# Second phase of a three-phase decoder layer: logits computed three query tiles ahead, the masked minimum placed ahead of the low part

## The chip, the cores and the metric

The kernel runs on one core of a Trainium2 chip. The metric is device time in microseconds (us) from one launch, median of repeated runs. The engines are named as the profile names them: PE is TensorE (PEld its weight loads), DVE is VectorE, ACT is ScalarE, POOL is GpSimd, and SP issues most of the transfers. Each engine runs its own list of instructions in the order in which the code issues them; semaphores tie the lists together.

## The reference, cut to what matters

The layer has three parts over 16 batches of 512 tokens with 512 features: a linear attention with a short convolution, a cross attention against a memory sequence, and a gated recurrence over the batch axis. The change is in the second part alone. With `xn` and `mn` the normalised tokens and memory, 4 query heads and one key/value head of 128 features:

```python
q = jnp.einsum('BTD,NDH->BTNH', xn, q_w)
kv = jnp.einsum('BSD,cKDH->cBSKH', mn, kv_w)
k, v = (kv[0], kv[1])
q = _apply_rope(q, q_pos) * HEAD_DIM ** (-0.5)
k = _apply_rope(k, k_pos)
logits = jnp.einsum('BTKGH,BSKH->BKGTS', q, k, preferred_element_type=jnp.float32)
masked = jnp.where(mem_mask[:, None, None, None, :], logits, MASK_FILL)
probs = jax.nn.softmax(masked, axis=-1).astype(x.dtype)
enc = jnp.einsum('BKGTS,BSKH->BTKGH', probs, v).reshape(B, T, NUM_HEADS, HEAD_DIM)
return jnp.einsum('BTNH,NHD->BTD', enc, out_w)
```

Before it, the memory's rows are scaled by the inverse root of their mean square; the sums of squares for that are the "memory's squares" of the change.

## The kernel before, in words

Every matrix operand is kept as two fp32r tensors, a high part (rounded on ACT) and a low part (the rest, subtracted on DVE), and `product` (lines 126 to 130, its three matmuls at L130, L131 and L132) multiplies high by high, high by low and low by high. The three phases follow each other; `phase_b` is the second.

**The pipeline.** `pipeline3` runs `step(s, new, old, fin)` for s = 0 to 17. In step s, batch s (`new`) has its keys, values and queries made, batch s-1 (`old`) goes through the softmax, and batch s-2 (`fin`) is finished and projected out. The memory of batch s+1 (`after`) is prepared at the end of step s. Steps 2 to 15 have all three batches; step 1 has no `fin`, step 16 no `new`.

**The slots.** A step has J = 16 slots, j = 0 to 15, one for each tile of 128 queries by 512 keys of `old` (4 heads by 4 tiles). Each engine has its own loop over j, and the order in these loops is written out by hand. What a tile goes through:
- PE `logits(b, j)`: one product into one of two PSUM banks, `logit_banks[j % 2]`. It waits until the tile that stood there two before has been read: `earlier(top_sb, b, j, 2)`.
- DVE `masked(b, j)` (L1393, L1394): adds the mask, takes the negated minimum, and writes the tile to one of four places in SBUF (`soft`, `SLOTS = 4`). Its second instruction, the read of the accumulator, posts `top_sb`.
- ACT `exp` (L1248), DVE `one_over` (L1383, a reciprocal), POOL `normalise` (L1200).
- PE `turn_p(j)` (L1580): four transposes into the single PSUM bank `pT_bank`. It waits for `normalise` and until the low part of the tile before has been read out of that bank.
- ACT `p_high` (L1257) and DVE `p_low` (L1402) split that bank, and PE `encode` (tile b_e) multiplies four such tiles by the values.

In a slot of PE `logits` comes first, then the work of that slot (keys and values at slots 0 and 2, the output at 3 to 6, `encode`, the queries at 8, 9, 11 and 12, the turning of the memory at 13 and 14), and `turn_p(j)` last. On DVE a slot is `one_over(j+1)`, `p_low(j-1)`, `masked(j+2)`, then the rest. The memory of `after` is turned on PE in slots 13 and 14, rounded on ACT in slots 14 and 15 (`memory_high`, L1128), and its low parts are made on DVE in slots 14 and 15 (`memory_low`, L1132), each waiting for its high part.

Two of the lines that matter below, in PE's `logits` and in DVE's `masked`:

```python
if free := earlier(top_sb, b, j, 2):
    pe.wait_ge(*free)
```

Of the kernel before, what the change touches and what calls it, by code (L numbers as in the profile page):

```python
# [189 lines left out]
class Kernel:  # L190
# [728 lines left out]
    def phase_b(self, ctx):  # L919
# [2 lines left out]
        BIG = 2.0 ** 100  # L922
        HALF = HD // 2
        J = H * T
        SLOTS = 4
        with ExitStack() as held:
            sb = lambda n, s, d=F32: self.sb(ctx, f"b_{n}", s, d)
            ev = lambda n, per=1, unit=1: Event(ctx, nc, f"b_{n}", per, unit)
# [226 lines left out]
            def tile(b, j):  # L1155
                return (b * J + j) % SLOTS

# [85 lines left out]
            def scalar(act):  # L1243
                def step(s, new, old, fin):
# [56 lines left out]
                    after = new.b + 1 if following(new, B) else None  # L1301
                    for j in range(J):
# [46 lines left out]
                        if s == 0 and 2 <= j <= 5:  # L1349
                            output_weight_high(act, j - 2)  # L1350
                        if after:
                            if 3 <= j <= 6:
                                square(act, after, j - 3)
                            if j == 8:
                                mem_apply(act, after, 0)
                                mem_apply(act, after, 1)
                            if j == 10 or j == 11:
                                mem_apply(act, after, j - 8)
# [17 lines left out]
            def vector(dve):  # L1376
                dve.wait_ge(params.sem, params.upto(0))

                def step(s, new, old, fin):
                    def one_over(b, j):  # L1380
                        at = tile(b, j)
                        dve.wait_ge(p_exp.sem, p_exp.upto(b, j))
                        dve.reciprocal(one_in_sum[:, at:at + 1], row_sum[:, at:at + 1]).then_inc(sum_one.sem, sum_one.unit)  # L1383

                    def masked(b, j):

                        at = tile(b, j)
                        dve.wait_ge(logit_ps.sem, logit_ps.upto(b, j))
                        if free := earlier(pT_ps, b, j, SLOTS):
                            dve.wait_ge(*free)  # L1390
                        if j == 0:
                            dve.wait_ge(mask_f.sem, mask_f.upto(b))
                        dve.memset(carrier[:, at:at + 1], 0.0)  # L1393
                        dve.tensor_tensor_reduce(out=soft[:, at, :], in0=logit_banks[j % 2][:, :], in1=mask_row[b % 2][:, :],  # L1394
                                                 scale=-1.0, scalar=3e38, op0=ALU.add, op1=ALU.min,
                                                 accum_out=minus_top[:, at:at + 1]).then_inc(top_sb.sem, top_sb.unit)
# [58 lines left out]
                    after = new.b + 1 if following(new, B) else None  # L1455
                    for j in range(J):
                        if old and j < J - 1:
                            one_over(old.b, j + 1)
                        if new and j == J - 1:
                            one_over(new.b, 0)  # L1460
                        if old and j >= 1:
                            p_low(old.b, j - 1)
                        if fin and j == 0:
                            p_low(fin.b, J - 1)
                        if after and j == 15:
                            memory_low(dve, s, after, 2)
                            memory_low(dve, s, after, 3)
                        if old and j < J - 2:
                            masked(old.b, j + 2)
                        if new and j >= J - 2:  # L1470
                            masked(new.b, j - J + 2)
                        if fin:
                            if j == 0:
                                enc_low(fin.b, 2)
# [83 lines left out]
            def tensor(pe):  # L1558
                def step(s, new, old, fin):
# [75 lines left out]
                        mm.then_inc(q_ps.sem, q_ps.unit)  # L1635

                    for j in range(J):
                        if old and j < J - 2:
                            logits(old.b, j + 2)
                        if s == 0 and j == J - 2:  # L1640
                            pe.wait_ge(self.a_x1.sem, self.a_x1.upto(B - 1))
                        if new and j >= J - 2:
                            logits(new.b, j - J + 2)
                        if new and j == 0:
                            keys_values(0)
                        if fin and j == 1:
# [654 lines left out]
```

## Time and profile before

| what | us |
|---|---|
| median of 3 runs (3152.20 to 3154.09) | 3153.61 |
| the profiled execution | 3155.96 |
| its span, first to last instruction | 3154.2 |
| PE busy | 3115.6 (99%) |
| DVE busy | 1778.2 (56%) |
| ACT busy | 1297.7 (41%) |
| POOL busy | 836.5 (27%) |
| TensorE clock granted, mean | 0.997 |

The profiled execution has 1.8 us outside its span and is 2.35 us above the median of the runs. The chain that ended last is PE for 96% of the span. The second phase runs from about 924 us to about 1895 us of the span. A full step of it takes 60.69 us. In timelines a row's first number is the start in us from the span's start, the second its length; "x4" merges four instructions in a row; square brackets at the end give the engine's idle time before the row and what ended it. "PEclk" is the granted clock, 1.00 for 2.4 GHz and 0.50 for 1.2 GHz.

### The profile page before, as it was taken

The page shows a single profiled execution, that of the slowest core. Times are in us where ns is not written, and L with a number is a line of the kernel's source. Part 1 is how long each engine was busy: PE and PEld are TensorE (multiplying, and loading weights), DVE is VectorE, ACT ScalarE, POOL GpSimd, SP SyncE. Part 2 cuts the span into 40 slices and gives each one's busy share as a digit, 9 for nine tenths or more (in the row PEclk, how much of TensorE's full clock was granted, in tenths as well). Part 3 has the DMA queues.
Part 4 walks back from the last instruction along what each step waited for, and adds up shares of the span by engine and source line. Part 5 has one row for each costly group of instructions (what it writes and reads, how often), then busy time and mean ns, then how long its engine had stood idle before and what let it go on. Part 6 is the DMA issues. An engine that isn't in the chain of part 4 may idle for free.

```text
span 3154.2 us, 41122 instructions
## 1 busy us (share of the span) xinstructions
PE 3115.6 (99%) x15828; PEld 2630.9 (83%) x15828; DVE 1778.2 (56%) x3901; ACT 1297.7 (41%) x2475; POOL 836.5 (27%) x699
## 2 busy tenths in 40 slices
PE   8999999999989999999999989999999999999999
PEld 7888888888878888888888878888888888888887
DVE  6666665757577877777787766232232232221355
ACT  4333333333446766766666653222222212221243
POOL 0101010100146666666666650000000000000144
PEclk9999999999999999999999999999999999999999
DMA  3121121212222112211211232000001000010386
GB/s 111 41 72 50 48 73 41 81 41 94 72 99 81 57 68 78 72 69 55 95 69 55 80 103 86 27 27 27 27 31 50 27 27 27 27 54 17 122 292 227
DMA packets 118802, 220.76 MB, mean 70 GB/s; under 512 B 7504, under 2 KB 13648, under 8 KB 118608
## 3 DMA queue, kind: packets, MB, share of 16 engines
q1 hardware_dynamic: 118608, 218.14, 20.2%
q8 instruction: 126, 2.06, 0.3%
q14 instruction: 68, 0.56, 0.1%
HBM read 152.06 MB, written 66.06 MB: 69 GB/s over the span
## 4 chain that ended last, share of the span: by engine, by line
PE 96%; DVE 1%; ACT 1%; issue 1%; DMA 0%; POOL 0%; SPq 0%; DVEq 0%; ACTq 0%
PE c_p L132 11%; PE c_p L131 11%; PE c_p L130 11%; PE a_p L130 6%; PE a_p L132 5%; PE a_p L131 5%; PE b_n L132 5%; PE b_n L130 5%; PE b_n L131 5%; PE b_t L1580 3%; PE d_p L130 2%; PE d_p L132 2%; PE d_p L131 2%; PE a_r L130 2%; PE a_r L132 2%; PE a_r L131 2%
## 5 line engine op out<-in xcount | busy, mean ns | idle before, releaser
L1200 POOL TENSOR_SCALAR b_soft<-b_soft,b_one_in_sum 128x512 f32<-128x512 f32 x256 | 401.2, 1568 | 299.8 <-DVE b_one_in_sum L1383 299.8
L1800 ACT ACTIVATE c_gate<-c_p,c_bias 128x512 f32<-128x512 f32 x180 | 124.2, 690 | 718.3 <-PE c_p L132 718.3
L1834 DVE TENSOR_TENSOR c_gate<-c_gate,c_gate 128x512 f32<-128x512 f32 x64 | 44.3, 692 | 524.0 <-ACT c_gate L1800 524.0
L1402 DVE TENSOR_TENSOR b_p_lo<-b_t,b_p_hi 128x512 fp32r<-128x512 f32 x256 | 175.1, 684 | 159.8 <-ACT b_p_hi L1257 157.2
L1248 ACT ACTIVATE b_soft<-b_soft,b_minus_top 128x512 f32<-128x512 f32 x256 | 185.2, 723 | 180.7 <-DVE b_minus_top L1394 176.1
L344 POOL TENSOR_TENSOR kept_scale<-c_ln_ve,minus_half 128x4 f32<-128x4 f32 x16 | 16.1, 1009 | 898.5 <-DVE c_ln_ve L336 898.5
L551 ACT ACTIVATE a_elu<-a_p 128x512 f32<-128x512 f32 x128 | 76.5, 598 | 353.0 <-PE a_p L132 353.0
L344 POOL TENSOR_TENSOR a_ln_sc<-a_ln_ve,minus_half 128x4 f32<-128x4 f32 x16 | 16.3, 1017 | 695.6 <-DVE a_ln_ve L336 695.6
L1257 ACT ACTIVATE b_p_hi<-b_t 128x512 fp32r<-128x512 f32 x256 | 151.7, 592 | 108.6 <-PE b_t L1580 108.6
L1394 DVE CUSTOM_DVE_ANT_0 b_soft<-b_l,b_mask_row 128x512 f32<-128x512 f32 x256 | 175.2, 684 | 0.0
L1580 PE MATMUL b_t<-ident,b_soft 128*128 128x128 f32 x1024 | 155.7, 275 | 10.7 <-DVE b_p_lo L1402 9.6
L2024 POOL TENSOR_TENSOR d_x<-d_x,d_y 128x512 f32<-128x512 f32 x60 | 79.8, 1332 | 260.5 <-ACT d_y L2041 260.4
L1580 PEld LDWEIGHTS b_t<-ident,b_soft 128*128 128x128 f32 x1024 | 123.0, 142 | 29.7 <-DVE b_p_lo L1402 14.6
L130 PE MATMUL b_l<-b_k_hi,b_q_hi 128*128 128x512 f32 x256 | 122.7, 479 | 0.0
L667 DVE SCALAR_TENSOR_TENSOR a_q<-a_p,a_elu 128x512 f32<-128x512 f32 x64 | 44.2, 691 | 134.3 <-ACT a_elu L553 134.3
L1836 DVE TENSOR_TENSOR c_gate<-c_gate,c_c_f 128x512 f32<-128x512 f32 x64 | 44.2, 691 | 122.8 <-ACT c_gate L1800 122.8
L130 PE MATMUL a_p<-a_Wk_hi,a_xT_hi 128*128 128x512 f32 x256 | 105.3, 411 | 0.1
L130 PE MATMUL a_p<-a_Wv_hi,a_xT_hi 128*128 128x512 f32 x256 | 104.1, 407 | 0.0
L130 PE MATMUL a_r<-a_Wp_hi,a_z_hi 128*128 128x512 f32 x256 | 102.9, 402 | 0.0
L130 PE MATMUL b_e<-b_p_hi,b_v_hi 128*128 128x512 f32 x256 | 101.0, 395 | 0.8 <-DVE b_enc_lo L1407 0.8
L132 PE MATMUL b_l<-b_k_hi,b_q_lo 128*128 128x512 f32 x256 | 101.6, 397 | 0.0
L130 PE MATMUL c_p<-c_nT_hi,c_wf_hi 128*128 128x512 f32 x256 | 101.0, 395 | 0.0
(286 smaller groups left out, 9614.8 us busy)
## 6 DMA issues: line engine op xcount, KB each, us to landing
a_res<-in_x SPq DMA_DIRECT2D x16, 1024.0 KB, 5.9
x<-a_res SPq DMA_DIRECT2D x16, 1024.0 KB, 5.2
b_mem<-in_ctx SPq DMA_DIRECT2D x16, 1024.0 KB, 5.3
b_x<-x SPq DMA_DIRECT2D x16, 1024.0 KB, 5.6
b_res<-x SPq DMA_DIRECT2D x16, 1024.0 KB, 5.6
x<-b_res SPq DMA_DIRECT2D x16, 1024.0 KB, 4.5
c_x<-x SPq DMA_DIRECT2D x16, 1024.0 KB, 5.8
d_x<-x SPq DMA_DIRECT2D x16, 1024.0 KB, 6.6
```

The source lines that it names most:

```text
L130: pe.matmul(out, stationary.high, moving.high, start=first, stop=False)
L131: pe.matmul(out, stationary.high, moving.low, start=False, stop=False)
L132: return pe.matmul(out, stationary.low, moving.high, start=False, stop=last)
L551: act.activation(elu[:, u % 2, :], bank[:, :], ACT.Relu, scale=-1.0).then_inc(elu_exp.sem, elu_exp.unit)
L1200: pool.tensor_scalar(soft[:, at, :], soft[:, at, :], one_in_sum[:, at:at + 1], None, ALU.mult).then_inc(p_norm.sem, p_norm.unit)
L1248: act.activation(soft[:, at, :], soft[:, at, :], ACT.Exp, bias=minus_top[:, at:at + 1], scale=-1.0, accum_out=row_sum[:, at:at + 1]).then_ ...
L1257: act.activation(p[h % 2].high[:, :, t * P:(t + 1) * P], pT_bank[:, :].rearrange("p (i s) -> p i s", i=T), ACT.Copy).then_inc(p_hi.sem, p_ ...
L1394: dve.tensor_tensor_reduce(out=soft[:, at, :], in0=logit_banks[j % 2][:, :], in1=mask_row[b % 2][:, :], scale=-1.0, scalar=3e38, op0=ALU.a ...
L1402: dve.tensor_tensor(part.low, pT_bank[:, :].rearrange("p (i s) -> p i s", i=T), part.high_f32(), ALU.subtract).then_inc(p_lo.sem, p_lo.unit)
L1580: mm = pe.transpose(pT_bank[:, i * P:(i + 1) * P], soft[:, tile(old.b, j), i * P:(i + 1) * P], self.ident[:, :])
L1800: act.activation(gate[j % 2][i][:, :], gating.banks[(3 * j + i) % 6][:, :], ACT.Tanh if g == "c" else ACT.Sigmoid, bias=added[:, i, j:j + ...
L2024: pool.tensor_tensor(x[old.par][:, t, :], x[old.par][:, t, :], y[:, t % 2, :], ALU.add).then_inc(out_sb.sem, out_sb.unit)
```

## The change

Four edits, all in `phase_b`:
- PE computes `logits` three tiles ahead instead of two (`AHEAD = 3`). The first tiles of the new batch thus stand in slots 13, 14 and 15 of its step. There are still two PSUM banks for the logits and four places in `soft`.
- DVE's `masked(j+2)` stands ahead of `p_low(j-1)` in slots 0 to 14. In slot 15 `masked(new, 1)` stays behind `memory_low`.
- In step 1 alone, ACT's squares of the memory stand in slot 2 (three) and slot 3 (one) instead of one in each of slots 3 to 6.
- `memory_low` in slot 15 is written at another place of the loop, with the same neighbours as before.

```diff
--- before.py
+++ after.py
@@ -922,7 +922,7 @@
         BIG = 2.0 ** 100
         HALF = HD // 2
         J = H * T
-        SLOTS = 4
+        SLOTS, AHEAD = 4, 3
         with ExitStack() as held:
             sb = lambda n, s, d=F32: self.sb(ctx, f"b_{n}", s, d)
             ev = lambda n, per=1, unit=1: Event(ctx, nc, f"b_{n}", per, unit)
@@ -1349,7 +1349,13 @@
                         if s == 0 and 2 <= j <= 5:
                             output_weight_high(act, j - 2)
                         if after:
-                            if 3 <= j <= 6:
+                            if s == 1 and j == 2:
+                                square(act, after, 0)
+                                square(act, after, 1)
+                                square(act, after, 2)
+                            if s == 1 and j == 3:
+                                square(act, after, 3)
+                            if s != 1 and 3 <= j <= 6:
                                 square(act, after, j - 3)
                             if j == 8:
                                 mem_apply(act, after, 0)
@@ -1458,17 +1464,19 @@
                             one_over(old.b, j + 1)
                         if new and j == J - 1:
                             one_over(new.b, 0)
+                        if old and j < J - 2:
+                            masked(old.b, j + 2)
+                        if new and j == J - 2:
+                            masked(new.b, 0)
                         if old and j >= 1:
                             p_low(old.b, j - 1)
                         if fin and j == 0:
                             p_low(fin.b, J - 1)
-                        if after and j == 15:
+                        if after and j == J - 1:
                             memory_low(dve, s, after, 2)
                             memory_low(dve, s, after, 3)
-                        if old and j < J - 2:
-                            masked(old.b, j + 2)
-                        if new and j >= J - 2:
-                            masked(new.b, j - J + 2)
+                        if new and j == J - 1:
+                            masked(new.b, 1)
                         if fin:
                             if j == 0:
                                 enc_low(fin.b, 2)
@@ -1635,12 +1643,12 @@
                         mm.then_inc(q_ps.sem, q_ps.unit)
 
                     for j in range(J):
-                        if old and j < J - 2:
-                            logits(old.b, j + 2)
-                        if s == 0 and j == J - 2:
+                        if old and j < J - AHEAD:
+                            logits(old.b, j + AHEAD)
+                        if s == 0 and j == J - AHEAD:
                             pe.wait_ge(self.a_x1.sem, self.a_x1.upto(B - 1))
-                        if new and j >= J - 2:
-                            logits(new.b, j - J + 2)
+                        if new and j >= J - AHEAD:
+                            logits(new.b, j - J + AHEAD)
                         if new and j == 0:
                             keys_values(0)
                         if fin and j == 1:
```

PE at the seam of two steps, before. The first two rows are the last `turn_p` of step 1; the names b_l0 and b_l1 are the two logit banks, and b_n is the bank that takes keys and values:

```order
L1580 MATMUL b_t0<-ident_49,b_soft_183 128x128 [waits b_p_norm,b_p_lo]
L1580 MATMUL b_t0<-ident_49,b_soft_183 128x128 x3
L130 MATMUL b_l0<-b_k1_hi_188,b_q_hi_175 128x512 [waits b_top_sb]
L131 MATMUL b_l0<-b_k1_lo_189,b_q_hi_175 128x512
L132 MATMUL b_l0<-b_k1_hi_188,b_q_lo_176 128x512
L130 MATMUL b_n2<-b_kvw_hi_170,b_nT_hi_172 128x256 [waits b_memT_lo]
L131 MATMUL b_n2<-b_kvw_lo_171,b_nT_hi_172 128x256
```

and after, at the same seam:

```order
L1588 MATMUL b_t0<-ident_49,b_soft_183 128x128 [waits b_p_norm,b_p_lo]
L1588 MATMUL b_t0<-ident_49,b_soft_183 128x128 x3
L130 MATMUL b_l1<-b_k1_hi_188,b_q_hi_175 128x512 [waits b_top_sb]
L131 MATMUL b_l1<-b_k1_lo_189,b_q_hi_175 128x512
L132 MATMUL b_l1<-b_k1_hi_188,b_q_lo_176 128x512
L130 MATMUL b_n2<-b_kvw_hi_170,b_nT_hi_172 128x256 [waits b_memT_lo]
L131 MATMUL b_n2<-b_kvw_lo_171,b_nT_hi_172 128x256
```

The product behind the last `turn_p` is tile 2 in bank b_l0 before, and tile 3 in bank b_l1 after. The wait on b_top_sb is for tile 0 before and for tile 1 after; keys and values are behind it in both.

DVE in slot 14 of step 1 (`one_over`, `p_low`, then `masked` of the new batch's tile 0), before:

```order
L1383 RECIPROCAL b_one_in_sum_212<-b_row_sum_211 128x1 [waits b_p_exp]
L1402 TENSOR_TENSOR b_p1_lo_180<-b_t0,b_p1_hi_179 128x4x128 [waits b_p_hi]
L1393 MEMSET b_carrier_209 128x1 [waits b_mask_f,b_pT_ps,b_logit_ps]
L1394 ISA b_soft_183,b_minus_top_210<-b_l0,b_mask_row1_206 128x512
L1394 ISA b_minus_top_210 128x1
```

and after:

```order
L1389 RECIPROCAL b_one_in_sum_212<-b_row_sum_211 128x1 [waits b_p_exp]
L1399 MEMSET b_carrier_209 128x1 [waits b_mask_f,b_pT_ps,b_logit_ps]
L1400 ISA b_soft_183,b_minus_top_210<-b_l0,b_mask_row1_206 128x512
L1400 ISA b_minus_top_210 128x1
L1408 TENSOR_TENSOR b_p1_lo_180<-b_t0,b_p1_hi_179 128x4x128 [waits b_p_hi]
```

`masked` (the rows with b_carrier, b_soft and b_minus_top) has moved ahead of `p_low` (b_p1_lo), and both are behind `one_over` (b_one_in_sum). The next slot of DVE, slot 15 of step 1, after:

```order
L1389 RECIPROCAL b_one_in_sum_212<-b_row_sum_211 128x1 [waits b_p_exp]
L1408 TENSOR_TENSOR b_p1_lo_180<-b_t0,b_p1_hi_179 128x4x128 [waits b_p_hi]
L1132 TENSOR_TENSOR b_nT_lo_173<-b_n0,b_nT_hi_172 128x512 [waits b_memT_hi]
L1132 TENSOR_TENSOR b_nT_lo_173<-b_n1,b_nT_hi_172 128x512 [waits b_memT_hi]
L1399 MEMSET b_carrier_209 128x1 [waits b_pT_ps,b_logit_ps]
L1400 ISA b_soft_183,b_minus_top_210<-b_l1,b_mask_row1_206 128x512
L1400 ISA b_minus_top_210 128x1
```

These rows stand in the same order before: `masked` of tile 1, the one that PE's first product of the next step waits for after the change, is behind `p_low` and the two `memory_low` (b_nT_lo).

ACT in step 1, from `p_high` of slot 2 on, before:

```order
L1257 ACTIVATE b_p0_hi_177<-b_t0 128x4x128 [waits b_pT_ps]
L1248 ACTIVATE b_soft_183,b_row_sum_211<-b_soft_183,b_minus_top_210 128x512 [waits b_top_sb]
L1257 ACTIVATE b_p0_hi_177<-b_t0 128x4x128 [waits b_pT_ps]
L1270 ACTIVATE b_v1_hi_192<-b_n0 128x256 [waits b_kv_ps]
L1248 ACTIVATE b_soft_183,b_row_sum_211<-b_soft_183,b_minus_top_210 128x512 [waits b_top_sb]
L1031 ACTIVATE b_unused_sq0_207,b_sumsq_213<-b_mem_181 128x512 [waits b_sq,b_ms,b_mem_in]
L1257 ACTIVATE b_p0_hi_177<-b_t0 128x4x128 [waits b_pT_ps]
L1278 ACTIVATE b_nT_hi_172<-b_n1 128x512 [waits b_kv_ps,b_xT_ps]
```

and after:

```order
L1257 ACTIVATE b_p0_hi_177<-b_t0 128x4x128 [waits b_pT_ps]
L1248 ACTIVATE b_soft_183,b_row_sum_211<-b_soft_183,b_minus_top_210 128x512 [waits b_top_sb]
L1031 ACTIVATE b_unused_sq0_207,b_sumsq_213<-b_mem_181 128x512 [waits b_sq,b_ms,b_mem_in]
L1031 ACTIVATE b_unused_sq1_208,b_sumsq_213<-b_mem_181 128x512 [waits b_sq]
L1031 ACTIVATE b_unused_sq0_207,b_sumsq_213<-b_mem_181 128x512 [waits b_sq]
L1257 ACTIVATE b_p0_hi_177<-b_t0 128x4x128 [waits b_pT_ps]
L1270 ACTIVATE b_v1_hi_192<-b_n0 128x256 [waits b_kv_ps]
L1248 ACTIVATE b_soft_183,b_row_sum_211<-b_soft_183,b_minus_top_210 128x512 [waits b_top_sb]
```

The first three squares (b_unused_sq) now stand in a row between an `exp` and the next `p_high`.

## Rows read from the trace of the kernel before

**Rows 1.** Busy time by stage. Columns are named in the first line; (x) counts instructions.
```profile
core 0: us, PE busy (x) PEld busy (x) DVE busy (x) ACT busy (x) POOL busy (x), PEclk, DMA share, GB/s
924.00:955.00 31.00, 24.83 (x146) 20.05 (x145) 26.17 (x77) 20.58 (x48) 24.00 (x22) 0.94 0.20 67
955.00:1825.00 870.00, 870.00 (x4865) 746.16 (x4864) 683.72 (x1858) 580.32 (x1238) 563.41 (x470) 1.00 0.20 70
1825.00:1895.00 70.00, 61.55 (x321) 48.66 (x320) 47.14 (x126) 38.64 (x82) 33.44 (x23) 0.95 0.35 121
1895.00:3150.00 1255.00, 1253.24 (x5695) 1040.91 (x5693) 418.46 (x716) 314.06 (x524) 95.97 (x76) 1.00 0.20 68
```

**Rows 2.** Waits of PE in 924 to 955: total, times, longest.
```profile
PE b_t L1580 <- DVE b_p_lo L1402: 3.2, 4, 1.5
```

**Rows 3.** Waits of PE in 1825 to 1895.
```profile
PE b_t L1580 <- DVE b_p_lo L1402: 6.3, 6, 1.6
```

**Rows 4.** Timeline of PE at the seam of steps 1 and 2.
```profile
980.50 0.60 PE L1580 MATMUL b_t<-ident,b_soft 128*128 128x128 f32 x4
...
983.02 0.60 PE L1580 MATMUL b_t<-ident,b_soft 128*128 128x128 f32 x4
983.38 0.48 PE L130 MATMUL b_l<-b_k_hi,b_q_hi 128*128 128x512 f32 x1
```

**Rows 5.** Timeline of ACT at the same seam.
```profile
981.14 0.60 ACT L1257 ACTIVATE b_p_hi<-b_t 128x512 fp32r<-128x512 f32 x1
981.63 1.08 ACT L1128 ACTIVATE b_nT_hi<-b_n 128x512 fp32r<-128x512 f32 x2
```

**Rows 6.** Timeline of DVE at the same seam.
```profile
981.77 0.69 DVE L1402 TENSOR_TENSOR b_p_lo<-b_t,b_p_hi 128x512 fp32r<-128x512 f32 x1
982.38 1.28 DVE L1132 TENSOR_TENSOR b_nT_lo<-b_n,b_nT_hi 128x512 fp32r<-128x512 f32 x2
...
984.19 0.08 DVE L1394 DVE_READ_ACCUMULATOR2_ANT b_minus_top<- 128x1 f32 x1
```

**Rows 7.** Timeline of PE and DVE at the seam of steps 14 and 15.
```profile
1772.30 0.48 PE L130 MATMUL b_l<-b_k_hi,b_q_hi 128*128 128x512 f32 x1
...
1773.12 0.09 DVE L1394 DVE_READ_ACCUMULATOR2_ANT b_minus_top<- 128x1 f32 x1
```

**Rows 8.** Timeline at the seam of steps 0 and 1.
```profile
928.62 0.28 PE L130 MATMUL b_n<-b_kvw_hi,b_nT_hi 128*128 128x256 f32 x1
...
930.50 0.08 DVE L1394 DVE_READ_ACCUMULATOR2_ANT b_minus_top<- 128x1 f32 x1
...
933.16 0.55 PE L1580 MATMUL b_t<-ident,b_soft 128*128 128x128 f32 x3 [1.09 <-POOL b_soft L1200]
```

**Rows 9.** Timeline in step 1, from one turn_p to the next.
```profile
944.07 0.69 DVE L1402 TENSOR_TENSOR b_p_lo<-b_t,b_p_hi 128x512 fp32r<-128x512 f32 x1 [0.38 <-ACT b_p_hi L1257]
...
944.81 0.66 PE L1580 MATMUL b_t<-ident,b_soft 128*128 128x128 f32 x4 [1.50 <-DVE b_p_lo L1402]
...
945.41 0.72 ACT L1248 ACTIVATE b_soft<-b_soft,b_minus_top 128x512 f32<-128x512 f32 x1 [0.89 <-DVE b_minus_top L1394]
...
946.13 0.61 ACT L1031 ACTIVATE b_unused_sq<-b_mem 128x512 bf16<-128x512 f32 x1
...
946.75 0.58 ACT L1257 ACTIVATE b_p_hi<-b_t 128x512 fp32r<-128x512 f32 x1
...
948.10 0.69 PE L1580 MATMUL b_t<-ident,b_soft 128*128 128x128 f32 x2 [0.38 <-DVE b_p_lo L1402]
```

**Rows 10.** Timeline of PE in step 16, turn_p of slots 11 to 15.
```profile
1876.59 0.66 PE L1580 MATMUL b_t<-ident,b_soft 128*128 128x128 f32 x4 [1.32 <-DVE b_p_lo L1402]
...
1879.27 1.12 PE L1580 MATMUL b_t<-ident,b_soft 128*128 128x128 f32 x4 [1.32 <-DVE b_p_lo L1402]
...
1882.74 1.05 PE L1580 MATMUL b_t<-ident,b_soft 128*128 128x128 f32 x4
...
1889.84 0.66 PE L1580 MATMUL b_t<-ident,b_soft 128*128 128x128 f32 x4 [0.98 <-DVE b_p_lo L1402]
```

## The prediction

> **What bounds the kernel now.** The page first: PE is busy for 99% of the span and the chain that ended last is PE for 96% of it. So a change pays only if it takes idle time from PE, and costs whatever idle time it gives to PE. Next, the second phase by stage [rows 1]. Between 955 and 1825 us PE is busy for 870.00 of 870.00 us at a granted clock of 1.00. The two ends are different: 6.17 us idle in 924 to 955 (step 0's end and step 1), 8.45 us idle in 1825 to 1895 (step 15's end and step 16), and the mean clock is 0.94 and 0.95 there. The third view is the waits of PE in those two stretches: 3.2 and 6.3 us of them end with p_low [rows 2, 3], that is, turn_p waits for its single PSUM bank. The last view is the timeline at the places that the order of instructions points at, below.
>
> The reader is to see two things: all that the change can win lies in two stretches that together hold 14.6 us of idle time, and in the 870 us between them it can only lose.
>
> **Part 1: the seam of two steps.** PE's first instruction of a step is, after the change, the product of tile 3. It waits for the read of tile 1, since both use the second logit bank. DVE reads tile 1 in slot 15, and that order is untouched: p_low, two memory_low, then masked. Before, PE's first product is tile 2 and waits for tile 0, read a slot earlier.
>
> When is PE there, and when is tile 1 read? At the seam of steps 1 and 2, PE is done with turn_p(15) and starts its product at 983.38 [rows 4]. DVE's read of the accumulator, which posts tile 1, ends at 984.19 + 0.08 = 984.27 [rows 6]. A matmul that waits for DVE starts 0.05 us after DVE's instruction ends (944.07 + 0.69 = 944.76, then 944.81) [rows 9]. So PE starts at 984.32 instead of 983.38: 0.94 us idle.
>
> Can tile 1 be read earlier once the products are earlier? Its product is, by a whole slot, but that is not what holds it. What does is turn_p(14) at 980.50 [rows 4]: p_high follows at 981.14, memory_high at 981.63 [rows 5], p_low at 981.77, memory_low twice from 982.38 (0.60 apart), and masked behind them [rows 6]. The chain starts on PE in slot 15 itself, and PE's work from turn_p(14) to the step's end is as long as before (one product, two parts of encode, turn_p: 2.88 us from 980.50 to 983.38), against 3.77 us for the chain. A stall does not cure the next one: all engines shift together, as the period of 60.69 us a step (983.38 to 1772.30 over 13 steps [rows 4, 7]) is the same for all now. And nothing on PE that could run stands ahead of the waiting product: keys and values, behind it, are held up too.
>
> How often? The last seam with memory work, steps 14 and 15, has the same distance: 1773.12 + 0.09 against 1772.30 [rows 7], 0.91 + 0.05 = 0.96. There are 14 such seams, after steps 1 to 14; step 15 prepares no memory, and the seam after step 0 is counted in part 2. Price 14 x 0.94 = 13.2 us. PE has no idle time there in which it could vanish, so all of it is on the path. Bounds: 14 x 0.94 from below as long as the chain stands; above, 14 x 1.1 = 15.4 if the restart costs another 0.1 to 0.2 on a few. If the wait weren't there: 0.
>
> Other waits on the logit banks in a step are hidden: the read of a tile stands one slot of DVE before the product that needs it, with nothing as long as the memory's work ahead of it, and the shortest slot of PE in a full step is 2.5 us long (980.50 to 983.02 [rows 4]). I take 0.
>
> **Part 2: step 0's end and step 1.** The seam of steps 0 and 1 has the same wait, larger. Keys and values started at 928.62, and turn_p(0) waited 1.09 us for POOL until 933.16 [rows 8]; that makes 933.16 - 1.09 - 928.62 = 3.45 us of work with some waiting of its own in it. After the change PE has the product of tile 3 ahead of them, which waits for tile 1 until 930.50 + 0.08 + 0.05 = 930.63 [rows 8]; with 0.7 us for the product and 2.9 to 3.4 for the rest turn_p(0) is at 934.3 to 934.8, where 1.1 us of waiting was before. That is a loss of 1.1 to 1.6 us. I take 1.1.
>
> Then the gain. In slots 4 to 6 of step 1 one turn_p follows the other after 948.10 - 944.81 = 3.29 us, and the loop between them is p_low, masked, exp (945.41), square (946.13), p_high (946.75), p_low, turn_p [rows 9]. Masked ahead of p_low, and the squares out of these slots, cut it to turn_p to p_high 0.64, p_high to p_low 0.63 [rows 4 to 6], p_low to turn_p 0.74 [rows 9]: 2.01 us. But DVE has four instructions of some 0.61 each in such a slot (masked, p_low, the tokens' low part, a query's sum or the like), so I take 2.5. Three intervals give 3 x 0.79 = 2.4 us. Against it stand 0.5 us because the three squares in a row (each holds ACT for 0.62, 946.13 to 946.75) put 1.9 us ahead of p_high in slot 2, where turn_p(3) also waits for DVE's normalising of the tokens. Sum: 1.1 + 0.5 - 2.4 = -0.8 us. Bounds: the idle time of 6.17 and 0.06 x 31 x 1 = 1.9 us of clock are all that can be won; lost can be 1.6 + 1.9 + a second spell of the low clock, 1.7. From -8 to +5; the value lies near zero because DVE, not PE, is what these slots then wait for.
>
> **Part 3: step 16.** Here masked ahead of p_low does what it did in step 1. From slot 11 to slot 13 turn_p follows at 2.68 and 3.47 us [rows 10], with waits of 1.32 each for p_low. The floor is again 2.01. Slot 11 has the same wait as slot 12, so the three intervals are 2.68 + 2.68 + 3.47 = 8.8 us and become 6.0: 2.8 us. Of the 8.45 - 2 x 1.32 = 5.8 us of idle time that is left, and of slots 14 and 15 (7.10 us from 1882.74 to 1889.84), I take about four tenths, 2.4 us: part of it waits for the gate weights' low parts, for which the change does nothing, and where DVE is late masked now delays p_low by 0.61. Sum -5.2 us. Bounds: 0, and 8.45 + 0.05 x 70 = 11.9.
>
> **Part 4: edits at no cost.** The squares of the other steps, the normalising, all transfers and POOL's list are where they were. Masked ahead of p_low in the full steps delays p_low by at most 0.61 where DVE is late, and turn_p behind it has 0.56 us to spare even in the shortest slot (p_low ends at 982.46, turn_p starts at 983.02 [rows 4, 6]), where masked moves nothing: 0. Without that cover it would be rival D.
>
> **The sum** for the profiled execution: 3155.96 + 13.2 - 0.8 - 5.2 = 3163.2. The median of the runs is 2.35 us lower: 3160.8.
>
> **A rule to weigh.** In 1895 to 3150 the clock stays at 1.00 with 1.8 us of idle time in all; in 924 to 955, with 6.17 us idle in 31, it is 0.94 [rows 1]. The Trainium skill, page "TensorE: Matmul & The Clock Gate", section "A second HAM failure mode: psum-queue depth-cycling", says that short, frequent idles of PE between groups of matmuls over PSUM banks can make the clock swing between its two levels. By that rule the seams, a bank's wait once a step, would pay twice; rival C prices it. The trace speaks against it here: one idle of 0.94 in 61.6 us is far rarer than what stands in 924 to 955.
>
> **The rivals.**
> A. The seam's wait isn't there, or is small: masked of tile 1 ends before PE arrives, because what feeds DVE comes forward more than I see. For it: the product of tile 1 and exp of tile 0 both come earlier. Against: the chain runs through turn_p(14) [rows 4 to 6]. Time 3153.6 - 6.0 = 3147.6, faster than before. It decides if slot 15's chain shrinks by 0.9 of its 3.77 us.
> B. The stalls are there, but the ends give more: all loops reach 2.01, the low clock of both stretches (1.9 and 3.5 us) goes. Start -3, end -9: 3153.6 + 13.2 - 12 = 3154.8, within 0.2%.
> C. Every seam costs a spell of the lower clock. In 924 to 955 the 0.06 of 31 us are 1.9 us lost; 14 x 1.9 = 26 more: about 3187.
> D. DVE is the next bound in the full steps, since p_low is late: turn_p waits in a slot or two of each step, 14 x 0.3 = 4 more: 3165.
>
> **How the numbers follow.** The forecast (seams plus small gains at the ends) 0.68, with a range of its own from 3157.5 to 3164.5; A 0.11, B 0.12, C 0.03, D 0.06. 0.2% is 6.3 us, about what a measurement of this kernel can tell from no change: slower begins at 3159.9. Of the forecast 0.11 lies below that, so slower is 0.57 + 0.03 + 0.06 = 0.66; A is half beyond the bound, faster 0.06; the rest, 0.28, is the same. The range 3155 to 3166 takes in the forecast's own, part of B and D, and leaves out A and C.
>
> **What the profile after would show.** Waits of PE b_l for DVE b_minus_top, 14 of about 0.9 us and one of 2 to 3 us at some 928, where before there is none; PE busy 870 of some 883 us in the middle stretch; steps of 61.6 us instead of 60.7; turn_p in slots 11 to 13 of step 16 some 2.0 us apart; step 1 about as long as before. Wrong I am if PE shows no wait for b_minus_top at the seams, or if the middle keeps its 60.69 us a step.

## The result: 3163.4 us, slower by 0.3%, and the profile after

| | before | after |
|---|---|---|
| median of 8 runs, us | 3153.61 (3151.58 to 3154.09) | 3163.44 (3162.83 to 3165.43) |
| ratio, 95% interval | | 1.0032 [1.0023, 1.0041] |
| profiled execution, us | 3155.96 | 3163.65 |
| its span, us | 3154.2 | 3161.9 |

The changed kernel is slower by 9.8 us where the forecast said 7.2; by the interval of the ratio the difference lies between 7.3 and 12.9 us. The page of the profile after, its first lines:

```profile
span 3161.9 us, 41122 instructions
...
PE 3114.1 (98%) x15828; PEld 2628.3 (83%) x15828; DVE 1785.1 (56%) x3901; ACT 1291.4 (41%) x2475; POOL 836.6 (26%) x699
```

PE does the same 15828 instructions and is busy for 3114.1 us, 1.5 less than before, so the time went into idle time of PE. Where it stands, by the stages of [rows 1] (the columns are those), with the bounds moved to where the stages now lie:

```profile
924.00:955.00 31.00, 25.45 (x162) 20.89 (x161) 27.34 (x83) 21.22 (x51) 25.72 (x24) 1.00 0.23 81
955.00:1838.00 883.00, 873.07 (x4858) 746.23 (x4858) 688.54 (x1855) 573.58 (x1238) 562.77 (x469) 1.00 0.20 68
1838.00:1906.00 68.00, 60.11 (x332) 48.10 (x331) 50.13 (x133) 39.63 (x84) 33.49 (x23) 1.00 0.35 124
1906.00:3160.00 1254.00, 1249.90 (x5676) 1038.39 (x5674) 415.61 (x706) 312.47 (x521) 94.91 (x76) 1.00 0.20 69
```

The middle, where PE had no idle time at all, now has 9.93 us of it. The waits of PE between 955 and 1840 (total, times, longest) name it:

```profile
PE b_l L130 <- DVE b_minus_top L1400: 9.9, 14, 0.7
```

and between 924 and 955, beside the waits for p_low [rows 2], one for the read:

```profile
PE b_t L1588 <- DVE b_p_lo L1408: 3.2, 5, 1.0
PE b_l L130 <- DVE b_minus_top L1400: 2.3, 1, 2.3
```

The seam of steps 1 and 2 again, first PE, then ACT and DVE, the places of [rows 4 to 6]:

```profile
978.90 0.60 PE L1588 MATMUL b_t<-ident,b_soft 128*128 128x128 f32 x4
...
981.42 0.60 PE L1588 MATMUL b_t<-ident,b_soft 128*128 128x128 f32 x4
982.73 0.50 PE L130 MATMUL b_l<-b_k_hi,b_q_hi 128*128 128x512 f32 x1 [0.71 <-DVE b_minus_top L1400]
```

```profile
979.54 0.60 ACT L1257 ACTIVATE b_p_hi<-b_t 128x512 fp32r<-128x512 f32 x1 [0.43 <-PE b_t L1588]
980.03 1.08 ACT L1128 ACTIVATE b_nT_hi<-b_n 128x512 fp32r<-128x512 f32 x2
```

```profile
980.17 0.69 DVE L1408 TENSOR_TENSOR b_p_lo<-b_t,b_p_hi 128x512 fp32r<-128x512 f32 x1 [0.58 <-ACT b_p_hi L1257]
980.78 1.28 DVE L1132 TENSOR_TENSOR b_nT_lo<-b_n,b_nT_hi 128x512 fp32r<-128x512 f32 x2
981.98 0.69 DVE L1400 CUSTOM_DVE_ANT_0 b_soft<-b_l,b_mask_row 128x512 f32<-128x512 f32 x1
...
982.59 0.08 DVE L1400 DVE_READ_ACCUMULATOR2_ANT b_minus_top<- 128x1 f32 x1
```

From turn_p(14) to the posted read is 978.90 to 982.67, 3.77 us, the same as before. PE's product would follow turn_p(15) after 0.36 us [rows 4], at 981.78, and starts at 982.73, 0.95 later. The row shows only 0.71 of it as idle, since the end of the transposes ahead of it is modelled. A reader who adds up the idle time (9.9 us in 14 waits) is some 3.8 us short of what the waits cost (13.7 us, below).

To see the cost whole, I measure from one turn_p to the next, all from the starts of turn_p in the traces. The mark for the first seam is an instruction of step 0 on DVE, first before, then after. On DVE nothing ahead of it was changed. On PE the product of tile 0 now stands ahead of it in time, but that doesn't move the mark: it comes 6.61 us after the first BATCH_NORM_STATS2 of its group before (917.91) and 6.62 after (917.53).

```profile
924.52 0.68 DVE L326 BATCH_NORM_STATS2 b_ln_st<-b_x 128x6 f32<-128x512 f32 x1
```

```profile
924.15 0.68 DVE L326 BATCH_NORM_STATS2 b_ln_st<-b_x 128x6 f32<-128x512 f32 x1
```

A star says that PE's clock fell in that part of that profile; "again" is a second profile of the kernel before, and e1 to e8 are the experiments below. A step goes from turn_p(15) to turn_p(15).

| us | before | again | after | e7 | e3 | e2 | e1 | e8 |
|---|---|---|---|---|---|---|---|---|
| mark to turn_p(0) of step 1 | 8.64 | 8.65 | 9.79 | 9.79 | 8.64 | 9.20 | 8.66 | 8.63 |
| step 1, turn_p(0) to (15) | 49.87* | 51.26* | 47.48 | 50.05 | 52.30* | 47.46 | 48.03 | 48.01 |
| one of steps 2 to 14 | 60.69 | 60.69 | 61.66 | 61.65 | 60.80 | 61.06 | 60.77 | 60.76 |
| step 15 | 60.14 | 60.15 | 61.20 | 61.23 | 60.81 | 60.60 | 60.71 | 60.28 |
| step 16 | 57.75* | 55.80 | 53.32 | 55.65 | 56.70* | 53.34 | 52.71 | 53.31 |
| turn_p(15) of step 16 to the end | 1264.34 | 1264.35 | 1264.35 | 1264.38 | 1264.36 | 1264.35 | 1264.38 | 1264.35 |

After against before, in the order of the rows: +1.15 at the first seam, -2.4 in step 1, 13 x 0.97 = +12.6, +1.1 in step 15, -4.4 in step 16, 0 behind it. With the mark itself 0.4 earlier this is +7.7, the difference of the spans (3161.9 - 3154.2).

### The profile page after: what moved, and what is told of

Its sections match the earlier page's. It is cut to its first block, busy times and chain, and to the rows that moved or that the text cites. A ratio compares the mean times of both kernels' runs of the same rounds, so it can differ in the third digit from the quotient of the medians.

```text
span 3161.9 us, 41122 instructions
## 1 busy us (share of the span) xinstructions
PE 3114.1 (98%) x15828; PEld 2628.3 (83%) x15828; DVE 1785.1 (56%) x3901; ACT 1291.4 (41%) x2475; POOL 836.6 (26%) x699
## 4 chain that ended last, share of the span: by engine, by line
PE 96%; DVE 2%; ACT 1%; issue 1%; DMA 0%; SPq 0%; DVEq 0%; ACTq 0%
PE c_p L132 11%; PE c_p L130 11%; PE c_p L131 11%; PE a_p L130 5%; PE a_p L132 5%; PE a_p L131 5%; PE b_n L132 5%; PE b_n L130 5%; PE b_n L131 5%; PE b_t L1588 3%; PE d_p L130 2%; PE d_p L132 2%; PE d_p L131 2%; PE a_r L130 2%; PE a_r L132 2%; PE a_r L131 2%
## 5 line engine op out<-in xcount | busy, mean ns | idle before, releaser
L130 PE MATMUL b_l<-b_k_hi,b_q_hi 128*128 128x512 f32 x256 | 122.7, 479 | 12.5 <-DVE b_minus_top L1400 12.2
L130 PE MATMUL c_p<-c_nT_hi,c_wc_hi 128*128 128x512 f32 x256 | 101.1, 395 | 0.0
```

The lines of the kernel that those rows point to most:

```text
L130: pe.matmul(out, stationary.high, moving.high, start=first, stop=False)
```

## The experiments

The kernels are named e1 to e8. "ratio" is to the kernel before, from runs on the same chip, with its 95% interval.

### e1: tile 1 read ahead of the low parts in slot 15

```diff
-                        if new and j == J - 2:
-                            masked(new.b, 0)
+                        if new and j >= J - 2:
+                            masked(new.b, j - J + 2)
                         if old and j >= 1:
                             p_low(old.b, j - 1)
 ...
-                        if new and j == J - 1:
-                            masked(new.b, 1)
```

> The changed kernel, but in slot 15 DVE reads tile 1 of the new batch ahead of p_low and of the two memory_low. Theory (the 9.8 us are 14 seams of 0.97 us in which PE waits for that read, 13.6 us, less what the ends give): the waits of PE b_l for b_minus_top go from 14 to 0 in the middle, a step is 60.7 us again, the seam of steps 0 and 1 waits about 0.9 instead of 2.3 us, and the time is 3163.4 - 13.6 - 1.4 = 3148.4, faster than before by 5. Rival 1 (the products three ahead cost by themselves, through the two banks or the order on PE): 3163 stays. Rival 2 (the wait only moves: memory's low parts come 0.6 to 1.2 us later and keys and values wait for them at the seam): a wait of PE b_n for b_nT_lo of 0.3 or more per seam, 3153 or above.

Measured: 3149.21 us (11 runs), ratio 0.9988 [0.9979, 0.9996], 14.2 less than after. The waits of PE for b_minus_top are gone between 955 and 1825, and the first one fell from 2.3 to 0.9 us, which costs nothing (8.66 us from the mark to turn_p(0)). Of the 1.13 us that are won there step 1 gives back 0.55 (48.03 instead of 47.48), since turn_p(1) now comes 2.75 us after turn_p(0) instead of 2.01; together with steps that are 0.08 longer than 60.69 this makes up the 0.8 us by which 3148.4 was missed. All waits of PE from 924 to 955:

```profile
PE b_t L1586 <- DVE b_p_lo L1408: 3.8, 5, 1.4
PE b_l L130 <- DVE b_minus_top L1400: 0.9, 1, 0.9
```

DVE at the seam, where the read now stands ahead of p_low and memory_low:

```profile
977.04 0.69 DVE L1400 CUSTOM_DVE_ANT_0 b_soft<-b_l,b_mask_row 128x512 f32<-128x512 f32 x1
977.66 0.09 DVE L1400 DVE_READ_ACCUMULATOR2_ANT b_minus_top<- 128x1 f32 x1
977.66 0.69 DVE L1408 TENSOR_TENSOR b_p_lo<-b_t,b_p_hi 128x512 fp32r<-128x512 f32 x1
978.26 1.28 DVE L1132 TENSOR_TENSOR b_nT_lo<-b_n,b_nT_hi 128x512 fp32r<-128x512 f32 x2
```

So the place of that one read is the cause of the loss, and with it moved the kernel beats both others, the one before by 0.12% (0.04 to 0.21).

### e2: one memory_low ahead of the read instead of two

```diff
                         if after and j == J - 1:
                             memory_low(dve, s, after, 2)
-                            memory_low(dve, s, after, 3)
                         if new and j == J - 1:
                             masked(new.b, 1)
+                        if after and j == J - 1:
+                            memory_low(dve, s, after, 3)
```

> The changed kernel, but only one of the two memory_low of slot 15 stays ahead of the read of tile 1. Theory: the chain to the read is one DVE instruction shorter (0.60 us), so the seam's cost falls from 0.97 to 0.37 us: 14 x 0.60 = 8.4 us less, and 0.6 less at the first seam, 3163.4 - 9.0 = 3154.4; a step is 61.1 us. Rival 1: no change, 3163. If the wait were set by something other than this chain (ACT, the product of tile 1), it would stay near 0.97 or vanish altogether.

Measured: 3155.07 us (11 runs), ratio 1.0003 [0.9994, 1.0012]. A step takes 61.06 us, 0.37 over 60.69; taking 0.60 us out of the chain took 0.60 out of the stall. PE and then DVE at the seam of steps 1 and 2:

```profile
981.59 0.60 PE L1589 MATMUL b_t<-ident,b_soft 128*128 128x128 f32 x4
982.30 0.50 PE L130 MATMUL b_l<-b_k_hi,b_q_hi 128*128 128x512 f32 x1
```

```profile
982.16 0.08 DVE L1400 DVE_READ_ACCUMULATOR2_ANT b_minus_top<- 128x1 f32 x1
```

The product starts 0.71 after turn_p(15) instead of 0.36, 0.06 after the read ends, yet the row has no bracket: the stall of some 0.35 us is wholly under the modelled end of the transposes. Only the step's length shows it.

### e3: masked ahead of p_low, logits two ahead as before

The kernel before with `AHEAD = 2` and DVE's order of the change:

```diff
+                        if old and j < J - 2:
+                            masked(old.b, j + 2)
+                        if new and j == J - 2:
+                            masked(new.b, 0)
                         if old and j >= 1:
                             p_low(old.b, j - 1)
 ...
-                        if old and j < J - 2:
-                            masked(old.b, j + 2)
-                        if new and j >= J - 2:
-                            masked(new.b, j - J + 2)
+                        if new and j == J - 1:
+                            masked(new.b, 1)
```

> The kernel before with one edit of the change alone: masked ahead of p_low in slots 0 to 14; products two ahead, squares as before. Theory: no seam waits, so the middle stays 60.69 us a step; the loop of turn_p in short slots (3.3 us in step 1, 2.7 in step 16) is cut to product 1.1 + masked 0.7 + p_low 0.7 = 2.6 us, less than with products three ahead: start -1 us, end -2 us, 3150.6. Rival (both edits are needed, since masked now waits for its product and holds p_low behind it): short slots of the full steps (13 and 14, 2.7 us) get waits too, 14 x 0.1 to 0.3 us, and the time is 3154 to 3157.

Measured: 3155.78 us (11 runs), ratio 1.001 [1.0001, 1.0018]. The theory, that DVE's order alone brings the gain at both ends, falls. In slots 4 to 6 of step 1 one turn_p follows the other after 2.75 to 2.81 us, where 2.6 was expected:

```profile
944.33 0.66 PE L1582 MATMUL b_t<-ident,b_soft 128*128 128x128 f32 x4 [0.96 <-DVE b_p_lo L1402]
947.14 0.66 PE L1582 MATMUL b_t<-ident,b_soft 128*128 128x128 f32 x4 [1.03 <-DVE b_p_lo L1402]
949.89 0.66 PE L1582 MATMUL b_t<-ident,b_soft 128*128 128x128 f32 x4 [0.89 <-DVE b_p_lo L1402]
```

With two tiles ahead, the product that `masked` reads is issued on PE behind the turn_p of the slot before. So `masked` waits for it, and p_low, now behind `masked`, waits too: product, masked and p_low stand in a row in that loop. (That is inferred from the order and the distances. The trace has 0.18 us of idle time on DVE ahead of the `masked` at 948.53 and none ahead of the one at 945.78, so DVE's own work is part of it.) Slots 4 to 6 fall from 3.29 us to these values, but slots 1 and 3, 2.14 and 2.17 us long before, rise to 2.75 and 2.70, and slots 11 and 12 of step 16 take 2.70 and 2.75, no less than before. Full steps are 0.11 us longer and step 15 is 0.67 longer, 13 x 0.11 + 0.67 = 2.1 us in all, about what the medians differ by (1.9). The rival of the expectation (both edits are needed, 3154 to 3157) held.

### e7: logits three ahead, DVE and ACT as before

```diff
-        SLOTS = 4
+        SLOTS, AHEAD = 4, 3
 ...
-                        if new and j >= J - 2:
-                            logits(new.b, j - J + 2)
+                        if new and j >= J - AHEAD:
+                            logits(new.b, j - J + AHEAD)
```

> The kernel before with PE's products three ahead alone; masked behind p_low and squares as before. Theory: the seam's cost is in this edit (14 x 0.97 = 13.6 us, 1.5 at the first seam) and the gain at the ends is in masked ahead of p_low, so here the cost stands without the gain: 14 waits of PE b_l for b_minus_top, turn_p 3.3 us apart in step 1 and 2.7 in step 16, 3153.8 + 15 = 3169. Rival (the early products themselves shorten the ends, order on DVE or not): 3164. Rival (the seam's cost comes only with DVE's new order): 3154.

Measured: 3168.68 us (5 runs), ratio 1.0051 [1.0038, 1.0063], 15 over before. Waits of PE from 955 to 1838:

```profile
PE b_l L130 <- DVE b_minus_top L1394: 10.0, 14, 0.7
```

The seams are lost in full and nothing is won: step 1 takes 50.05 (49.87 before), step 16 55.65 (55.80 before, profiled again). The terms add up to 1.15 + 0.2 + 12.5 + 1.1 - 0.15 = 14.8 us. Together with e3 this shows that the gain at the ends belongs to neither edit alone. It takes the product out of the loop (three ahead) and `masked` off the turn from p_high to p_low: only with both does step 16 fall to 53.3.

### e8: the read behind p_low, ahead of both memory_low

```diff
+                        if new and j == J - 1:
+                            masked(new.b, 1)
                         if after and j == J - 1:
                             memory_low(dve, s, after, 2)
                             memory_low(dve, s, after, 3)
-                        if new and j == J - 1:
-                            masked(new.b, 1)
```

> As the kernel that reads tile 1 first in slot 15 (3149.2), but with that read behind p_low and ahead of both memory_low. Theory: the chain from turn_p(14) to the read is then 0.64 + 0.63 + 0.61 + 0.77 = 2.65 us, 0.2 us less than PE's 2.88 to the seam, so there is still no wait, and p_low is not delayed by 0.61; the 0.05 to 0.08 us a step by which that kernel's step exceeds 60.69 us go: 14 x 0.06 = 0.8 us less, 3148.4. Rival (0.2 us isn't enough, since a wait ends some 0.05 to 0.1 late): waits of 0.05 at each seam, 3150.

Measured: 3149.52 us (11 runs), ratio 0.9988 [0.9979, 0.9996], the same as e1. Neither of the two expectations holds: 3148.4 didn't come, and the rival's waits of 0.05 us aren't there either, since PE waits for nothing between 955 and 1825. What it was to tell, whether the 0.08 us by which e1's steps are longer than 60.69 come from p_low being late by one `masked`, is answered with no: e8's steps are 0.07 longer too. In e1 the excess stands in slots 0 and 1 (0.03 and 0.06 us); its cause stays open.

### e5 and e6: the squares

e5 is the changed kernel without the edit of the squares, e6 the kernel before with it alone. The edit:

```diff
-                            if 3 <= j <= 6:
+                            if s == 1 and j == 2:
+                                square(act, after, 0)
+                                square(act, after, 1)
+                                square(act, after, 2)
+                            if s == 1 and j == 3:
+                                square(act, after, 3)
+                            if s != 1 and 3 <= j <= 6:
                                 square(act, after, j - 3)
```

> The changed kernel with the squares of step 1 back in slots 3 to 6, one each. Theory (DVE, with four instructions of 0.61 in such a slot, sets step 1 once masked is ahead): ACT has 2.3 to 2.8 us a slot with a square in it, against 2.5 on DVE, so turn_p of slots 4 to 6 follow at 2.5 to 2.8 instead of 2.07 to 2.8, and the time is 0.3 to 1 us above the changed kernel's 3163.4: 3164. Rival (the squares' place is what made step 1 shorter): 2 us or more above it, 3165.5.

> The kernel before with the squares' edit alone. Theory: the loop of turn_p in slots 4 to 6 of step 1 is p_low, masked, exp, square, p_high, and loses one square of 0.61 in each, from 3.29 to 2.68 us, while slot 3 gets 1.2 us more in front of p_high: 3 x 0.61 - 1.2 = 0.6 us less, 3153.2, no wait anywhere in the middle. Rival: no effect at all, since the loop is then set by DVE, 3153.8; or slot 3's delay outweighs it, 3154.5.

Measured: e5 3163.71 us (6 runs), ratio 1.0032 [1.0019, 1.0044]; e6 3152.96 us (11 runs), ratio 1.0 [0.9992, 1.0009]. Neither can be told from its partner by the time. By the traces step 1 takes 47.79 us in e5 against 47.48 after, and 49.74 in e6 against 49.87 before: 0.1 to 0.3 us. The edit does move work, as turn_p of slots 3 to 5 in step 1 of e6 shows:

```profile
943.07 0.66 PE L1586 MATMUL b_t<-ident,b_soft 128*128 128x128 f32 x4 [1.01 <-DVE b_p_lo L1408]
946.35 0.65 PE L1586 MATMUL b_t<-ident,b_soft 128*128 128x128 f32 x4 [1.51 <-DVE b_p_lo L1408]
949.03 0.66 PE L1586 MATMUL b_t<-ident,b_soft 128*128 128x128 f32 x4 [0.20 <-DVE b_p_lo L1408]
```

Slots 5 and 6 are shorter (2.68 for 3.29 us), but turn_p(3) comes 3.26 us after turn_p(2) where before it was 2.17: the squares' time in slot 2 takes back what the other slots gain.

### e4: the kernel before, profiled again

The same kernel, unchanged.

> The kernel before, unchanged, for a second profile. My sum for the profiled execution was right to 0.4 us (3163.2 against 3163.65) but the medians differ by 9.8 instead of 7.7 us. Theory: the profile of before held spells at 1.2 GHz in steps 1 and 16 (mean clock 0.94 and 0.95) that not every execution has, and cost it some 2.3 us. Then this profile may show fewer of them and a time near 3153.6. Rival: the profile adds 2.3 us to this kernel always: the same spells at the same places, 3156.

Measured: 3155.21 us, span 3153.5. Neither theory nor rival holds as written: the spells stand elsewhere than in the first profile, and the time is still 1.4 us above the median of the runs beside it (3153.86), as much as the spell at 935 costs (below). Windows 920 to 955 and 1870 to 1910, first of the profile of before, then of e4 (PEclk is the third number from the end):

```profile
920.00:955.00 35.00, 28.83 (x166) 23.37 (x165) 29.42 (x82) 23.32 (x53) 26.43 (x24) 0.95 0.17 59
1870.00:1910.00 40.00, 35.59 (x181) 29.02 (x182) 28.88 (x69) 17.40 (x36) 9.86 (x7) 0.91 0.25 90
```

```profile
920.00:955.00 35.00, 27.50 (x159) 22.47 (x158) 28.20 (x78) 22.62 (x52) 25.11 (x22) 0.95 0.16 55
1870.00:1910.00 40.00, 35.14 (x193) 28.06 (x194) 30.63 (x74) 18.14 (x38) 10.43 (x7) 1.00 0.29 100
```

One kernel, two executions: one has some 7 us at 1.2 GHz in step 16 (0.09 of 40 us, times two), the other none, and its step 16 is 1.95 us shorter (55.80 against 57.75). The profile after has PEclk 1.00 in the whole second phase (above). So 1.95 of the 4.4 us that step 16 seems to win are the cost of a spell that the kernel before has in one execution and not in another. The profile of e6 shows such a spell again: the clock is low at the same place (PEclk 0.91 in 1870 to 1910), and step 16 takes 57.68 us. Whether the change also makes the spell rarer is open: a spell stands in step 16 in three of the five profiles without both edits (before, e3, e6) and in none of the five with both (after, e1, e2, e5, e8), too few to tell.

## Why the prediction was right, and which terms were off

**The seam (part 1), right.** The wait, its place, its 14 occurrences and its chain are as forecast. It was put at 0.94 and measured 0.97 a step, 13.7 us in all (12.6 + 1.1) for 13.2 forecast, inside its bounds. "A stall does not cure the next one" held: the last seam costs what the first costs, and e1, e2 and e8 show that the instructions ahead of the read set the price.

**The first seam (part 2), right.** Forecast a loss of 1.1 us, measured 9.79 - 8.64 = 1.15. After the change tile 1 is read 5.98 us after the mark, as before (930.50 - 924.52 and 930.13 - 924.15), and PE's product waits for it:

```profile
930.13 0.08 DVE L1400 DVE_READ_ACCUMULATOR2_ANT b_minus_top<- 128x1 f32 x1
...
930.26 0.50 PE L130 MATMUL b_l<-b_k_hi,b_q_hi 128*128 128x512 f32 x1 [2.31 <-DVE b_minus_top L1400]
...
933.94 0.60 PE L1588 MATMUL b_t<-ident,b_soft 128*128 128x128 f32 x4
```

From product to turn_p(0) are 3.68 us, for 3.6 to 4.1 in the forecast. Of the 2.31 us of wait, 1.15 are lost: 1.09 were there already as the wait for POOL [rows 8].

**Step 1 (part 2), right.** Forecast 2.4 won and 0.5 lost, 1.9 together; measured 2.4 together, 2.5 won in slots 4 to 6 and 0.2 lost at turn_p(3) (2.38 us for 2.17), with 0.1 won in slot 1. The squares play a small part in it: without their edit (e5) slots 4 to 6 take 2.81, 2.49 and 2.38 us. The turn_p of slots 3 to 6, after:

```profile
942.39 0.66 PE L1588 MATMUL b_t<-ident,b_soft 128*128 128x128 f32 x4 [0.58 <-DVE b_p_lo L1408]
945.21 0.66 PE L1588 MATMUL b_t<-ident,b_soft 128*128 128x128 f32 x4 [1.02 <-DVE b_p_lo L1408]
947.70 0.66 PE L1588 MATMUL b_t<-ident,b_soft 128*128 128x128 f32 x4 [0.64 <-DVE b_p_lo L1408]
949.77 0.44 PE L1588 MATMUL b_t<-ident,b_soft 128*128 128x128 f32 x2 [0.29 <-DVE b_p_lo L1408]
```

They are 2.82, 2.49 and 2.07 apart instead of 3.29, 2.46 in the mean for the 2.5 forecast.

**Step 16 (part 3), mis-sized.** Forecast -5.2. The trace shows -4.4 against the profile of before, but -2.5 against e4, in which the clock does not fall. Slots 11 to 13 in e4:

```profile
1877.77 0.66 PE L1580 MATMUL b_t<-ident,b_soft 128*128 128x128 f32 x4 [1.32 <-DVE b_p_lo L1402]
...
1880.45 0.66 PE L1580 MATMUL b_t<-ident,b_soft 128*128 128x128 f32 x4 [1.32 <-DVE b_p_lo L1402]
...
1883.13 0.66 PE L1580 MATMUL b_t<-ident,b_soft 128*128 128x128 f32 x4 [0.64 <-DVE b_p_lo L1402]
```

Slots 11, 12, 14 and 15, after:

```profile
1887.46 0.66 PE L1588 MATMUL b_t<-ident,b_soft 128*128 128x128 f32 x4 [0.71 <-DVE b_p_lo L1408]
...
1889.53 0.66 PE L1588 MATMUL b_t<-ident,b_soft 128*128 128x128 f32 x4 [0.71 <-DVE b_p_lo L1408]
...
1893.67 0.66 PE L1588 MATMUL b_t<-ident,b_soft 128*128 128x128 f32 x4
...
1897.50 0.66 PE L1588 MATMUL b_t<-ident,b_soft 128*128 128x128 f32 x4 [0.93 <-DVE b_p_lo L1408]
```

The floor of 2.01 was right: 2.01 to 2.07 here. Two other things failed. "The three intervals are 2.68 + 2.68 + 3.47": the 3.47 us of slot 13 [rows 10] were 2.68 and a fall of the clock, as in e4 the slots 11 to 14 are 2.68 each; the three win 1.89, not 2.8. And of the remaining idle time four tenths, 2.4 us, were to be won; the slots other than 11 to 13 gave 0.6. Slots 14 and 15 together take 5.90 us after, 5.93 in e4 and 5.92 in e7, so something else than this loop bounds them: turn_p(14) comes 0.6 earlier, and turn_p(15) waits that much longer. The trace shows what it waits for. DVE, after:

```profile
1894.11 1.29 DVE L187 TENSOR_TENSOR c_ui_lo<-b_n,c_ui_hi 128x512 fp32r<-128x512 f32 x2 [0.49 <-ACT c_ui_hi L183]
1895.45 0.48 DVE L1546 MEMSET c_start_f<- 128x512 f32 x1
1895.97 0.88 DVE L1549 TENSOR_SCALAR c_start_f<-c_start_f,c_in 128x128 f32<-128x128 f32 x4
1896.76 0.69 DVE L1408 TENSOR_TENSOR b_p_lo<-b_t,b_p_hi 128x512 fp32r<-128x512 f32 x1
```

Work for the third phase (two low parts of the gate weights c_ui, then c_start_f) fills DVE from 1894.11 on without a gap ahead of the p_low that turn_p(15) waits for. In e4 the same instructions stand there, and from PE's turning of the gate weights (L178) to turn_p(15) it is 4.72 us after (1892.78 to 1897.50) and 4.75 in e4 (1884.31 to 1889.06). The forecast named the gate weights' low parts as a reason to take only a part, and still took too much. That moving this work would free slot 15 is not shown; no run has it.

**The sum.** 13.2 - 0.8 - 5.2 = 7.2 was forecast. Measured, with step 16 taken against e4: 1.15 - 2.4 + 13.7 - 2.5 = +9.95, and the medians differ by 9.8. The mis-sized term is part 3, by 2.7 us. That is the whole of the difference, since the other two misses (0.5 more at the seams, 0.4 less at the start) cancel. In the profiled execution it doesn't show (3163.2 forecast, 3163.65 measured) because before's profile held the low clock that makes up 1.95 of it: that the sum was right to 0.4 us there is luck. For the same reason the last step of the sum, "The median of the runs is 2.35 us lower", failed: the profiled execution after is 0.2 above its median, not 2.35. And that 9.95 meets the 9.8 of the medians so well is luck too, with an interval of 7.3 to 12.9 us.

**The rivals.** A (no wait) is refuted by the 14 waits, and its price by e1: without the wait 3149.2, not 3147.6. B (larger gains) came true in its signs but not in its price: in the profile after the clock is 1.00 at both ends and the loops of step 16 reach 2.01 to 2.07, yet the ends give 5.7 us (1.2 and 4.4, with the spell of before counted in) and not 12. C (a spell of the low clock at each seam) is refuted for the 14 seams: stalls of 0.97 us with a granted clock of 1.00 in 955 to 1838. Its price was too high as well, since the spell in step 1 from which it was taken cost nothing (below). The Trainium skill, page "TensorE: Matmul & The Clock Gate", section "A second HAM failure mode: psum-queue depth-cycling", says that short idles of PE between groups of matmuls, when they are frequent, can make the clock swing between its two levels. Here one idle every 61.7 us left it at 1.00. The first seam is another matter: in e5 the wait of 2.31 us is followed by a spell (PEclk 0.94 in 924 to 955), and from the mark to turn_p(0) it takes 11.30 us instead of 9.79; after the same wait the profile after has none. D (p_low late in full steps) does not show in after's steps, which are those of e7 (61.66 and 61.65), where masked stands behind p_low.

## What to carry to other kernels

Work issued further ahead needs its buffer freed earlier: find the instruction that frees it and what stands ahead of that one where the order is irregular (a seam, a first or last step), and move both together; here that turned 3163.4 into 3149.2. Measure a stall by the distance between two fixed instructions, not by the idle time in brackets. Before an interval that is longer than its neighbours is counted as a wait to be won, look whether the granted clock fell in it, and profile a second time if it did. And before a share of an idle time is counted as a gain, name the engine that ends it: in slot 15 of step 16 it was DVE with work of the next phase.

## What the runs showed of the hardware that I had not expected

The granted clock falls to 1.2 GHz at other places in each execution of one kernel: in about 946 to 950 and 1879 to 1885 us in one profile of before, in 935 to 939 alone of these stretches in the other, nowhere in either stretch after. What PE does before a spell doesn't decide it alone: ahead of the one at 1879 it waited 1.32 us for p_low twice, and the same two waits stand in e4 (1877.77 and 1880.45 above) with the clock at 1.00. The spell at 946 costs nothing (turn_p stays 3.29 us apart across it), that at 935 1.4 us (slot 2 takes 5.59 instead of 4.07, and slot 3 gives 0.16 back), that in step 16 1.95. Much of the spread of the kernel before goes with the clock. Here are 49 of its runs, sorted by the mean granted clock of each:

| mean clock | runs | mean time, us |
|---|---|---|
| 1.000 | 12 | 3152.5 |
| 0.999 | 24 | 3153.4 |
| 0.998 | 11 | 3154.5 |
| 0.997 | 2 | 3155.3 |

The mark of step 0 lies between 922.11 (e1) and 924.99 us (e6) in the ten profiles, though nothing that moves it was changed. A part of that goes with the clock, too: in the four profiles with PEclk 1.00 in 880 to 892 us (e1, e3, e7, e8) the mark is at 922.11 to 923.46, in the six with 0.72 or 0.86 at 922.72 to 924.99. Two profiled executions are thus comparable to some three microseconds only, unless the marks lie inside the changed phase.
